# Swin block on one core: the gathers of split q and k rows move one place later, behind the next send of row maxima

## The chip, the cores and the metric

The kernel runs on one core of a Trainium2 chip. The metric is the time of one execution on the device, in microseconds. Lower is better.

## The reference

A shifted-window transformer block over an input of 8 images of 16 x 128 tokens with 32 channels. Windows are 4 x 32 tokens, so an image has 16 windows of 128 tokens; there are 4 heads of 8 channels.

```
y   = roll(layernorm(x) * g1 + b1, (-2, -2))            # then cut into windows
q, k, v = y @ qkv_w + qkv_b                             # q scaled by 8 ** -0.5
p   = softmax(q @ k.T + bias(rpb) + mask)               # 128 x 128, per window and head
x   = x + roll(p @ v @ proj_w + proj_b, (2, 2))
out = x + gelu((layernorm(x) * g2 + b2) @ fc1_w + fc1_b) @ fc2_w + fc2_b
```

All of it is float32; the gelu is the exact one.

## The kernel before

**Pairs, places and passes.** A pair is two windows with their four heads: 1024 score columns. There are 64 pairs, 8 to an image. All engines run the same loop over pairs `p` (line 285 on SyncE), written out without branches; `b = p // 8` is the image whose attention runs, and `s = p % 8` is the place in the pass of that image. Two neighbouring pairs make a group `k = j // 2`.

**Scores are computed twice.** S1 (`scores_s1`, L908) gives scores with queries on partitions; VectorE takes the maximum of every row (L524). S2 (`scores_s2`, L937) gives the transposed scores, from which ScalarE takes the exponential (L736), and TensorE multiplies that with the values (L957). S1 runs four pairs ahead of S2. So that the S2 scores come out with the row maximum already subtracted, the maxima are two more rows of the operand `q_rows`: TensorE transposes the maxima of a group (`transpose_max`, L871), ScalarE rounds them to bf16 (`m_hi`, L731), VectorE forms the remainder (`m_mid`, L530), and SyncE writes both into `q_rows` with two DMAs of 4 KB (`send_max`, L262). The S2 scores of the group's first pair wait for both DMAs (`d_m`). At every even place the loop sends group `(p + 2) // 2`; TensorE makes the transposes of that group in pair `p` just before the S2 scores of pair `p`, which belong to the group sent two places earlier. A group has thus one group's time from its transpose to its use.

**Split rows.** q and k have to be as exact as float32 but the score matmuls are bf16. So each projected q and k is split in three bf16 parts (HIGH, MID, LOW), and `q_rows` and `k_rows` hold six slots per element: on the q side three HIGH, two MID, one LOW, on the k side the same in another order. The parts of image `n` go to a scratch in HBM (`scatter`, one DMA of 256 KB for each part, L250) and come back into their slots by `gather(n, part, q or k)` (L212): three DMAs for a HIGH, two for a MID, one for a LOW, each of 128 KB. All twelve go into one of three buffers. A gather waits for the scatter of its part (`d_scr`). The first S1 scores of an image wait for all its gathers.

**SyncE's queue.** SyncE issues all of these in program order, and a wait in that order holds up everything behind it. In the pass of image `b`, the rows of image `n = b + 2` are scattered and gathered, for `n` from 2 to 7, so in passes 0 to 5. The places in that pass: 2, 4 and 6 send groups `4b + 2`, `4b + 3`, `4b + 4`; place 3 resets two rows of the buffer (`clear_max`); place 4 scatters HIGH, place 5 MID, place 6 LOW. The gathers stand at places 5, 6 and 7 and, for LOW, at place 0 of the next pass, behind the send of group `4b + 5`. Place 1 loads an image of x. Image 1 has an order of its own (pairs -2 and 0), which is not touched.

Of the kernel before, what the change touches and what calls it, by code (L numbers as in the profile page):

```python
# [19 lines left out]
HIGH, MID, LOW = 0, 1, 2  # L20
# [23 lines left out]
def swin_kernel(nc, x, params, rel_i_in, rel_j_in, aux_in, scratch, rel_scratch, out):  # L44
# [3 lines left out]
    with ExitStack() as ctx:  # L48
# [125 lines left out]
        def img(b):  # L174
            return X[:, b * IMG:(b + 1) * IMG]
# [7 lines left out]
        def low_parts(n, i):  # L183
            return 2 * n + i if n else 1
# [14 lines left out]
        def gathered(n):  # L199
            return 16 * (13 * (n // NBUF) + (12 if n % NBUF else 0))  # L200

        def gather(eng, n, part, qk):
            eng.wait_ge(d_scr[part], 16 * (n + 1))
            if n >= NBUF:
                eng.wait_ge(s2_done, PPI * (n - NBUF + 1))
            else:
                eng.wait_ge((zero_q, zero_k)[qk][n], 1)
            for s in range(6):
                if SLOT_PARTS[qk][s] == part:
                    dst = (q_rows, k_rows)[qk][s:128:8, n % NBUF, :].rearrange("p (a n) -> p a n", n=512)  # L210
                    src = scratch[n % 2, part].rearrange("u a k e n -> k e (u a) n")[qk]
                    eng.dma_start(dst, src).then_inc(d_qk[n % NBUF], 16)  # L212
# [5 lines left out]
        def _(sp):  # L218
# [11 lines left out]
            def aux_rows(i):  # L230
                lo = 0 if i else ROW // 2
                sp.wait_ge(zero_q[i], 1)
                sp.dma_start(q_rows[AUX:128:8, i, lo:].bitcast(fp32), aux_in[0, :, lo // 2:]).then_inc(d_aux[i], 16)
                sp.wait_ge(zero_k[i], 1)
                sp.dma_start(k_rows[AUX:128:8, i, lo:].bitcast(fp32), aux_in[1, :, lo // 2:]).then_inc(d_aux[i], 16)
# [8 lines left out]
            def scatter(n, part):  # L244
                if n > 2:
                    sp.wait_ge(d_qk[(n - 2) % NBUF], gathered(n - 2))
                if n == 2:
                    sp.wait_ge(d_first, 192)
                sp.wait_ge((hi_done, mid_done, lo_done)[part], low_parts(n, 1) if part == LOW else 2 * n + 2)
                sp.dma_start(scratch[n % 2, part].rearrange("u a k e n -> (a k e) u n"),  # L250
                             parts[:, n % 2, part, :, :]).then_inc(d_scr[part], 16)

            def clear_max(n):
                sp.wait_ge(s2_done, PPI * (n - NBUF + 1))
                dst = q_rows[AUX:128:32, n % NBUF, :].bitcast(fp32)
                sp.dma_start(dst, aux_in[0, 0:1, :].to_broadcast([4, ROW // 2])).then_inc(d_qk[n % NBUF], 16)

            def send_max(k):
                b, wx = k // GW, k % GW
                for at, t, done in ((AUX, m_hi, mhi_done), (AUX + 32, m_mid, mmid_done)):  # L260
                    sp.wait_ge(done, k + 1)
                    sp.dma_start(q_rows[at:128:64, b % NBUF, wx * 1024:(wx + 1) * 1024],  # L262
                                 t[:, k % 2, :]).then_inc(d_m[k % 2], 16)
# [16 lines left out]
            for p in range(FIRST, PAIRS):  # L280
                b, s = p // PPI, p % PPI
                n = b + 2
                if p % 2 == 0 and 0 <= (p + 2) // 2 < GROUPS:
                    send_max((p + 2) // 2)
                if s == 0 and 2 <= b + 1 < B:
                    gather(sp, b + 1, LOW, 0)
                    gather(sp, b + 1, LOW, 1)
                if p == -2:
                    scatter(1, HIGH)
                    scatter(1, MID)  # L290
                    gather(sp, 1, HIGH, 0)
                if p == 0:
                    scatter(1, LOW)
                    gather(sp, 1, HIGH, 1)
                    gather(sp, 1, MID, 0)
                    gather(sp, 1, LOW, 0)
                    gather(sp, 1, LOW, 1)
                if p == 3:
                    aux_rows(2)
                if s == (1 if b else 3) and b + 4 < B:  # L300
                    sp.dma_start(img(b + 4), x[:, (b + 4) * IMG:(b + 5) * IMG]).then_inc(d_x[b + 4], 16)
                if 2 <= n < B:
                    if s == 3 and n >= NBUF:
                        clear_max(n)
                    if s == 4:
                        scatter(n, HIGH)
                    if s == 5:
                        scatter(n, MID)
                        gather(sp, n, HIGH, 0)
                    if s == 6:  # L310
                        scatter(n, LOW)
                        gather(sp, n, HIGH, 1)
                    if s == 7:
                        gather(sp, n, MID, 0)
                        gather(sp, n, MID, 1)
            for m in range(B - 1):
                sp.wait_ge(res_done, m + 1)
                sp.dma_start(out[:, m * IMG:(m + 1) * IMG], res[:, m % 2, :]).then_inc(d_out[m % 2], 16)
# [929 lines left out]
```

## Time and profile before

| | us |
|---|---|
| median of 3 runs | 230.57 (229.99 to 231.49) |
| the profiled execution's own time | 228.56 |
| its span, first to last instruction | 226.8 |

| engine | busy us | share of the span |
|---|---|---|
| TensorE, matmul | 202.2 | 89% |
| VectorE | 164.7 | 73% |
| ScalarE | 149.4 | 66% |
| GpSimd | 128.3 | 57% |

The rows further down come from that one profiled execution. Times in them are microseconds from the first instruction. The loop over pairs fills about 28 to 200 us of the span; what follows is the MLP of all images.

### The profile page before, as it was taken

The page shows a single profiled execution, that of the slowest core. Times are in us where ns is not written, and L with a number is a line of the kernel's source. Part 1 is how long each engine was busy: PE and PEld are TensorE (multiplying, and loading weights), DVE is VectorE, ACT ScalarE, POOL GpSimd, SP SyncE. Part 2 cuts the span into 40 slices and gives each one's busy share as a digit, 9 for nine tenths or more (in the row PEclk, how much of TensorE's full clock was granted, in tenths as well). Part 3 has the DMA queues.
Part 4 walks back from the last instruction along what each step waited for, and adds up shares of the span by engine and source line. Part 5 has one row for each costly group of instructions (what it writes and reads, how often), then busy time and mean ns, then how long its engine had stood idle before and what let it go on. Part 6 is the DMA issues. An engine that isn't in the chain of part 4 may idle for free.

```text
span 226.8 us, 10661 instructions
## 1 busy us (share of the span) xinstructions
PE 202.2 (89%) x4600; PEld 120.9 (53%) x4600; DVE 164.7 (73%) x253; ACT 149.4 (66%) x217; POOL 128.3 (57%) x116
## 2 busy tenths in 40 slices
PE   0888789999899979997999999999969999989884
PEld 0844434655566546655665666466646666443221
DVE  3896855767688666876897887777747767866874
ACT  7465457846686656766766885857636765577883
POOL 7775698272448942987389578624651083150850
PEclk9999958999999988999999999999999999999999
DMA  6816457544523540444246224513541000000233
GB/s 206 245 55 178 123 176 221 157 135 128 173 70 97 185 143 13 138 149 145 75 153 204 66 95 128 160 57 108 155 145 31 7 4 9 1 3 0 94 140 139
DMA packets 24294, 25.57 MB, mean 113 GB/s; under 512 B 3556, under 2 KB 21732, under 8 KB 24164
## 3 DMA queue, kind: packets, MB, share of 16 engines
q1 hardware_dynamic: 23496, 24.16, 34.2%
q10 hardware_dynamic: 752, 0.74, 1.2%
q8 instruction: 36, 0.59, 1.1%
q14 instruction: 10, 0.08, 0.1%
HBM read 16.24 MB, written 8.39 MB: 109 GB/s over the span
## 4 chain that ended last, share of the span: by engine, by line
issue 40%; POOL 38%; PE 8%; DVE 5%; ACT 4%; DMA 2%; ACTq 1%; POOLq 1%; DVEq 0%
POOL rstd L376 17%; POOL X L406 4%; POOL parts L394 4%; POOL yn L386 3%; POOL xc L368 3%; POOL X L411 3%; PE ps L974 3%; DMA X<-x_tok 2%; ACT q_rows L741 1%; POOL mean L356 1%; ACT k_rows L741 1%; POOL var L362 1%; PE pq L974 1%; DVE negm L524 1%; PE pav L1004 1%
## 5 line engine op out<-in xcount | busy, mean ns | idle before, releaser
L524 DVE TENSOR_REDUCE negm<-ps 128x8 f32<-128x1024 f32 x64 | 78.1, 1223 | 30.2 <-PE ps L908 29.6
L736 ACT ACTIVATE prob<-ps 128x1024 f32<-128x1024 f32 x64 | 65.5, 1023 | 31.2 <-PE ps L937 28.9
L376 POOL TENSOR_TENSOR rstd<-var,neghalf 128x16 f32<-128x16 f32 x16 | 47.4, 2963 | 16.0 <-DVE var L489 15.1
L922 PE MATMUL ps<-rel_j,id_b 96*32 96x512 bf16 x512 | 40.6, 388 | 2.7 <-DVE negm L524 1.6
L957 PE MATMUL pav<-prob,va 128*32 128x128 f32 x1024 | 42.0, 281 | 0.5 <-issue 0.5
L937 PE MATMUL ps<-q_rows,k_rows 64*64 64x128 bf16 x1024 | 27.4, 226 | 7.2 <-DMA q_rows<-m_mid 7.1
L957 PEld LDWEIGHTS pav<-prob,va 128*32 128x32 f32 x1024 | 24.4, 110 | 13.2 <-issue 6.8
L937 PEld LDWEIGHTS ps<-q_rows,k_rows 64*64 64x64 bf16 x1024 | 16.8, 108 | 26.3 <-issue 14.9
L908 PEld LDWEIGHTS ps<-k_rows,q_rows 64*64 64x64 bf16 x1024 | 22.5, 109 | 7.0 <-issue 0.9
L908 PE MATMUL ps<-k_rows,q_rows 64*64 64x128 bf16 x1024 | 25.6, 219 | 0.0
L884 PE MATMUL ps<-rel_i,ident_b 64*64 64x512 bf16 x256 | 25.4, 386 | 0.0
L394 POOL TENSOR_TENSOR parts<-rest,parts 128x512 bf16<-128x512 f32 x15 | 17.3, 1157 | 10.5 <-ACT parts L719 10.5
L356 POOL TENSOR_SCALAR mean<-ssum 128x16 f32<-128x16 f32 x11 | 2.8, 257 | 35.9 <-DVE ssum L471 35.6
L731 ACT ACTIVATE m_hi<-pq 16x128 bf16<-16x128 f32 x32 | 8.5, 266 | 21.5 <-PE pq L871 21.0
L922 PEld LDWEIGHTS ps<-rel_j,id_b 96*32 96x32 bf16 x512 | 13.5, 98 | 6.5 <-ACT prob L736 2.9
L530 DVE TENSOR_TENSOR m_mid<-pq,m_hi 16x128 bf16<-16x128 f32 x32 | 8.7, 270 | 10.6 <-ACT m_hi L731 9.5
L386 POOL TENSOR_TENSOR yn<-xc,rstd 128x512 f32<-128x512 f32 x13 | 13.6, 1047 | 1.0
L368 POOL TENSOR_TENSOR xc<-X,mean 128x512 f32<-128x512 f32 x12 | 12.6, 1048 | 1.7 <-DVE yn L504 0.8
L471 DVE TENSOR_REDUCE ssum<-X 128x16 f32<-128x512 f32 x16 | 10.9, 680 | 3.0 <-DMA X<-x_tok 2.8
L515 DVE SCALAR_TENSOR_TENSOR rest<-pq,qk_bias,parts 128x512 f32<-128x512 f32 x12 | 9.0, 746 | 4.1 <-ACT parts L713 4.1
L483 DVE TENSOR_REDUCE vsum<-sq 128x16 f32<-128x512 f32 x16 | 10.8, 678 | 0.9 <-ACT sq L702 0.6
L1058 PE MATMUL pch<-par,oT 128*128 128x128 f32 x64 | 10.5, 286 | 1.1 <-DVE oT L626 1.1
(134 smaller groups left out, 320.1 us busy)
## 6 DMA issues: line engine op xcount, KB each, us to landing
slots<-parts SPq DMA_DIRECT2D x21, 256.0 KB, 2.9
q_rows<-slots SPq DMA_DIRECT2D x42, 128.0 KB
k_rows<-slots SPq DMA_DIRECT2D x40, 128.0 KB
X<-x_tok SPq DMA_DIRECT2D x8, 256.0 KB, 3.9
y_tok<-res SPq DMA_DIRECT2D x7, 256.0 KB, 2.0
q_rows<-m_hi SPq DMA_DIRECT2D x32, 4.0 KB
q_rows<-m_mid SPq DMA_DIRECT2D x32, 4.0 KB
bias_parts<-rel_parts SPq DMA_DIRECT2D x3, 128.0 KB
```

Of the source, the lines that this page charges most:

```text
L368: pool.tensor_tensor(per_window(xc[:, i, :]), per_window(img(n)), mean[:, i, :].unsqueeze(2).to_broadcast([128, WPI, C]), ALU.subtract).th ...
L376: pool.tensor_tensor(rstd[:, i, :], var[:, i, :], neghalf[:], ALU.pow).then_inc(rstd_done[i], 1)
L386: pool.tensor_tensor(per_window(yn[:, i, :]), per_window(xc[:, i, :]), rstd[:, i, :].unsqueeze(2).to_broadcast([128, WPI, C]), ALU.mult).t ...
L394: pool.tensor_tensor(parts[:, n % 2, LOW, u, :], rest[:, u, :], parts[:, n % 2, MID, u, :], ALU.subtract).then_inc(lo_done, 1)
L471: dve.tensor_reduce(ssum[:, i, :], per_window(img(n)), AX.X, ALU.add).then_inc(sum_done[i], 1)
L524: dve.tensor_reduce(dst, first_home(j)[:].rearrange("p (a u n) -> p a u n", u=2, n=TOK), AX.X, ALU.max, negate=True).then_inc(max_done, 1)
L736: act.activation(prob[:, j % NPROB, :], ps2[:], ACT.Exp).then_inc(exp_done, 1)
L884: pe.matmul(home[64 * c:64 * (c + 1), 512 * e:512 * (e + 1)], ident_b[64 * e:64 * (e + 1), 64 * e:64 * (e + 1)], rel_i[64 * e:64 * (e + 1) ...
L908: mm = pe.matmul(home[64 * c:64 * (c + 1), 512 * e + at:512 * e + at + TOK], q_rows[64 * e:64 * e + 64, b % NBUF, half], k_rows[64 * e:64 ...
L922: pe.matmul(ps2[32 * c:32 * (c + 1), 512 * e:512 * (e + 1)], id3_b[0:96, :], rel_j[0:96, c, e].unsqueeze(2).to_broadcast([96, 2, 2, TOK]), ...
L937: mm = pe.matmul(ps2[64 * c:64 * (c + 1), 512 * e + at:512 * e + at + TOK], k_rows[64 * e:64 * e + 64, b % NBUF, half], q_rows[64 * e:64 * ...
L957: mm = pe.matmul(pav[32 * h:32 * (h + 1), 128 * (j % 4):128 * (j % 4 + 1)], va[:, b % 2, at:at + 32], prob[:, j % NPROB, src:src + 128], s ...
```

## The change

Four `gather` calls in SyncE's loop each move to a later place. HIGH of q goes from place 5 to place 6, behind the send of group `4b + 4` and the LOW scatter. HIGH of k goes from place 6 to 7. MID of k goes from place 7 to place 0 of the next pass, behind the send of group `4b + 5` and ahead of the LOW gathers. MID of q stays at place 7. Nothing else is changed; the number of DMAs, their sizes and their waits are the same.

```diff
                 if s == 0 and 2 <= b + 1 < B:
+                    gather(sp, b + 1, MID, 1)
                     gather(sp, b + 1, LOW, 0)
                     gather(sp, b + 1, LOW, 1)
...
                     if s == 5:
                         scatter(n, MID)
-                        gather(sp, n, HIGH, 0)
                     if s == 6:
                         scatter(n, LOW)
+                        gather(sp, n, HIGH, 0)
+                    if s == 7:
                         gather(sp, n, HIGH, 1)
-                    if s == 7:
                         gather(sp, n, MID, 0)
-                        gather(sp, n, MID, 1)
```

## Rows read from the trace of the kernel before

**Rows 1.** The page: busy time by engine; granted clock in 40 slices.

```profile
PE 202.2 (89%) x4600; PEld 120.9 (53%) x4600; DVE 164.7 (73%) x253; ACT 149.4 (66%) x217; POOL 128.3 (57%) x116
...
PEclk9999958999999988999999999999999999999999
```

**Rows 2.** Waits of TensorE: who waited for whom, us in total, times, longest.

```profile
PE ps L937 <- DMA q_rows<-m_mid: 7.1, 6, 1.8
```

**Rows 3.** TensorE in order of time: start, us, instructions, [idle before <- releaser].

```profile
75.57 0.42 PE L937 MATMUL ps<-q_rows,k_rows 64*64 64x128 bf16 x16 [0.44 <-DMA q_rows<-m_mid]
...
82.47 0.42 PE L937 MATMUL ps<-q_rows,k_rows 64*64 64x128 bf16 x16 [1.58 <-DMA q_rows<-m_mid]
...
93.73 0.28 PE L871 MATMUL pq<-par,negm 128*16 128x128 f32 x1
...
105.83 0.42 PE L937 MATMUL ps<-q_rows,k_rows 64*64 64x128 bf16 x16 [1.23 <-DMA q_rows<-m_mid]
...
115.53 0.28 PE L871 MATMUL pq<-par,negm 128*16 128x128 f32 x1
...
126.13 0.28 PE L871 MATMUL pq<-par,negm 128*16 128x128 f32 x1
...
130.93 0.28 PE L871 MATMUL pq<-par,negm 128*16 128x128 f32 x1
...
136.03 0.28 PE L871 MATMUL pq<-par,negm 128*16 128x128 f32 x1
...
167.08 0.28 PE L871 MATMUL pq<-par,negm 128*16 128x128 f32 x1
```

**Rows 4.** ScalarE in order of time: `m_hi` of groups 8 and 24.

```profile
69.93 0.27 ACT L731 ACTIVATE m_hi<-pq 16x128 bf16<-16x128 f32 x1 [0.69 <-PE pq L871]
...
157.91 0.27 ACT L731 ACTIVATE m_hi<-pq 16x128 bf16<-16x128 f32 x1 [0.69 <-PE pq L871]
```

**Rows 5.** SyncE's queue in order of time, passes 0 and 1.

```profile
49.63 0.54 SPq L262 DMA_DIRECT2D q_rows<-m_hi  x1
...
51.95 2.05 SPq L212 DMA_DIRECT2D k_rows<-slots  x1
...
57.64 0.54 SPq L262 DMA_DIRECT2D q_rows<-m_hi  x1
...
70.63 2.47 SPq L212 DMA_DIRECT2D q_rows<-slots  x3
73.14 0.54 SPq L262 DMA_DIRECT2D q_rows<-m_hi  x1
...
74.38 0.37 SPq L250 DMA_DIRECT2D slots<-parts  x1
74.84 1.86 SPq L212 DMA_DIRECT2D k_rows<-slots  x3
76.80 1.19 SPq L212 DMA_DIRECT2D q_rows<-slots  x2
78.08 2.00 SPq L212 DMA_DIRECT2D k_rows<-slots  x2
80.13 0.54 SPq L262 DMA_DIRECT2D q_rows<-m_hi  x1
...
83.26 0.54 SPq L262 DMA_DIRECT2D q_rows<-m_hi  x1
```

**Rows 6.** Waits of SyncE's queue: who waited for whom, us in total, times, longest.

```profile
SPq L212 <- DMA slots<-parts: 12.7, 6, 3.4
```

**Rows 7.** Gather issues of line L212: ns least/median/most, first and last start.

```profile
L212 SPq DMA_DIRECT2D k_rows<-slots x40: 538/587/2047, 34.1 to 168.7; - x40
```

**Rows 8.** DMA queues from 51.9 to 53.0 us: packets, MB, share of 16 engines.

```profile
q8 instruction: 1, 0.02, 9.4%
```

**Rows 9.** Two stretches: us, busy by engine, granted clock, DMA share, GB/s.

```profile
76.00:80.00 4.00, 4.00 (x108) 2.37 (x104) 2.84 (x3) 3.50 (x5) 3.57 (x4) 1.00 0.56 169
83.00:87.00 4.00, 4.00 (x83) 2.32 (x75) 1.88 (x2) 1.94 (x3) 0.00 (x0) 0.57 0.42 132
```

## The prediction

> **What bounds the kernel now.** I read the page first: TensorE is busy 89% of the span, and the granted clock is full except around two places [rows 1]. So what can be won without taking work away is TensorE's idle time and the time at the lower clock. The list of what each engine waited for gives TensorE one entry of this kind inside the loop: 7.1 us in six waits of the S2 scores for the row `m_mid` of a send of row maxima [rows 2]. The order in time of TensorE [rows 3] shows three of them, two in pass 1 and one, of 1.23 us, in pass 2. Those of pass 1: 0.44 us at 75.57, for the send of group 8 (place 6 of the pass, the early send), and 1.58 us at 82.47, for the send of group 9 (place 0 of the next pass, the late send). Of the six waits this is the only one for an early send; the other five are for late sends, one in every pass with gathers but pass 3.
>
> Why the sends are late is read on ScalarE and in SyncE's queue, side by side [rows 4, 5]. `m_hi` of group 8 is finished at 70.20 (69.93 + 0.27), but its send is issued at 73.14, right behind the three gathers HIGH 0 (70.63 + 2.47). The late send goes out at 80.13, behind seven gathers and one scatter that follow the early send; TensorE reached the scores of that group at 80.89 (82.47 - 1.58) and was let go at 82.47, 2.34 us after the issue began. SyncE itself waits: 12.7 us in six waits for the scatters, ahead of HIGH 0 [rows 6]. While it waits there, the early send stands behind it.
>
> **Part 1: HIGH 0 behind the early send.** The three DMAs, and the wait on the HIGH scatter, move past two small sends and the LOW scatter on SyncE's queue. The early send then starts when `m_hi` is ready, at 70.22 and not at 73.14 in pass 1. Its 0.44 us wait goes. The scatter wait of [rows 6] costs nothing any more, because SyncE first waits for `m_hi`, and by then the scatter has had that time to land; if it has not, the rest of that wait falls between the two sends. Nothing on another engine waits for HIGH 0 soon: the gathered rows are first read by the S1 scores at place 4 of the next pass, two sends later.
>
> **Part 2: HIGH 1 and MID 1 one place later.** HIGH 1 passes no send (place 6 to place 7). MID 1, two DMAs, moves past the late send. So the run between the two sends was scatter + 3 + 2 + 2 gathers and becomes scatter + 3 + 3 + 2. Nominal steps from [rows 5]: sends and gap 73.14 to 74.38, 1.24; scatter 0.46; three gathers 1.96 (74.84 to 76.80); two gathers 1.28. Now 1.24 + 0.46 + 1.96 + 2 x 1.28 = 6.2 us; after 1.24 + 0.46 + 2 x 1.96 + 1.28 = 6.9 us. Pass 1 with the change: late send at 70.22 + 6.90 = 77.12, scores let go 2.34 later at 79.46, wanted at 80.89 - 0.44 = 80.45: **1.0 us of slack**. In passes 0 to 4 the distance between the two TensorE transposes is the same once waits are taken out, so the slack is the same. The last pass is shorter: `m_hi` ready at 158.18 (157.91 + 0.27), late send 165.1, let go 167.46, wanted at 167.08 + 0.28 = 167.36, the end of the transpose ahead of it [rows 3, 4]: 0.1 us too late even at nominal.
>
> **What eats the slack: long issues.** A gather issue takes 0.54 us at least, 0.59 in the median, but up to 2.05 [rows 7]. The interval between the sends is now 8.01, 6.99, 7.12, 6.60, 7.51 and 6.67 us in the six passes (the first two stand in [rows 5], four more are read the same way), so 1.8, 0.8, 0.9, 0.4, 1.3 and 0.5 us over nominal. HIGH 0's own three issues are over by 0.7, 0.6, 0.7, 0.5, 0.0 and 1.1 (the second is 2.47 against 1.86). The longest issue, at 51.95 [rows 5], coincides with a packet on the instruction queue [rows 8]; I found such a packet at nearly all the others. As TensorE's instruction stream does not change, these come at the same points of its work.
>
> Low end: excess as now, HIGH 0 free of it. Waits 0.8 + 0 + 0 + 0 + 0.3 + 0.6 = 1.7 us. High end: HIGH 0's excess is added to the run. Waits 1.5 + 0.4 + 0.6 + 0 + 0.3 + 1.7 = 4.5 us. I take 2.6, nearer the low end, because two of the packets that lengthen HIGH 0 (passes 0 and 5) would then fall beside the small sends, whose issues keep to 0.5 us.
>
> The Trainium skill (Runtime: NRT & Kernel Launch, "Instruction fetch mechanics") holds the crossing of an instruction block to be mostly hidden. By that the excess would vanish and the waits would be 0.1 us, which is the full case below; the 2.05 us issue speaks against it.
>
> **Part 3: what stands behind the late send.** MID 1 adds 1.28 us ahead of the next send (group 4b + 6): late send to next send is now 3.13 us (80.13 to 83.26) and becomes 4.4. Let go at 4.4 + 2.34 = 6.75 after the late send's start; TensorE, let go at 2.34 and then working one group, 4.8 us (126.13 to 130.93 [rows 3]), wants it at 7.1. It fits with 0.4 us; long issues there may take it. I put 0.3 us in all; the ends are 0 and 0.9 (a half microsecond in two passes).
>
> **Part 4: the clock.** After the 1.58 us of idleness at 80.89 the granted clock fell; in 83 to 87 us it was 0.57 of full, where the levels are 1.2 and 2.4 GHz [rows 9]. Full speed would have saved up to 4 x 0.43 = 1.7 us there. That idleness shrinks to at most 0.4 us by the sum, so I take the 1.7 back as the likelier; the other end is 0, since another long wait kept its clock. The first fall, near 28 us, is before the change's places.
>
> **Sum.** 7.1 - 2.6 - 0.3 + 1.7 = 5.9 us. It is on the path: TensorE is the busy engine, and pass 3, which has no such wait, already shows the pace without one, 20.50 us from transpose to transpose (115.53 to 136.03) against 21.80 in pass 2 (93.73 to 115.53) with a wait of 1.2 [rows 3]. So no other engine takes the place of the wait there. The profiled execution took 228.56 us (span 226.8, 1.8 around it); 228.56 - 5.9 = 222.7. The median of the runs is 2.0 above that execution, so the forecast is **224.7 us**.
>
> **Rivals.**
> - *Full gain.* No long issue in the run hits a late send: 7.1 + 1.7 = 8.8, 221.8 us. For it: 1.0 us of slack in five passes. Against: excess over 1.0 in two of the six now. Chance 0.13.
> - *Half gain.* Upper waits (4.5 + 0.9) and no clock back: 1.7 us, 228.9; with one of the two, some 227. For it: eight gathers in a row give a fetch more to hit. Chance 0.20, half of it under 1%.
> - *No change.* SyncE's order isn't what holds the scores: the waits move to the next send or to another engine. Against it pass 3. 230.6 us, chance 0.08.
> - *Slower: the send's data queue behind the gathers.* Place: the late send, with 8 gathers of 128 KB and a 256 KB scatter ahead of it, 1.31 MB in 5.7 us of issue, 230 GB/s. If they drain at only the 169 GB/s moved from 76 to 80 us [rows 9], they take 7.8 us, and the send's data land 2.1 us later. Then the waits are 2.1 + 0.9 - 1.0 = 2.0 in five passes and 3.1 in the last, 13.1 against 7.1: 236.6 us. It decides from waits above 1.2 us a pass, that is a drain below about 200 GB/s. Against it: 169 is what was issued, not what could drain, and 2.34 us from issue to release is no longer behind seven gathers than behind three (75.57 - 73.14 = 2.43). Chance 0.06. The Trainium skill (DMA: Bandwidth & Descriptors, "Queues, rings and completion order") says that descriptors of one issuing queue are consumed in ring order on each DMA engine. By that rule this would happen whenever a backlog stands; the trace shows none so far.
>
> **How the numbers follow.** Forecast 0.53, full 0.13, half 0.20, none 0.08, slower 0.06. About 1% (2.3 us) is what a measurement of this kernel tells from no change. Faster: 0.53 + 0.13 + 0.10 = 0.76. Same: 0.10 + 0.08 = 0.18. Slower: 0.06. The range reaches from the full gain, 221.8, to the upper waits without the clock, 228.9, and leaves out the last two rivals and the edges.
>
> **What would show it.** Right: in SyncE's order the early send starts within 0.1 us of `m_hi`; 6.9 to 8.5 us between the two sends; TensorE's wait for `m_mid` falls from 7.1 to about 3 us, most of it in passes 0, 4 and 5; full clock in pass 1. Wrong: a wait for `m_mid` in pass 3, more than 2.4 us from the late send to its scores, a wait of the S1 scores for gathered rows, or a clock that falls elsewhere.

## The result and the profile after

| | before | changed |
|---|---|---|
| median, us | 231.03 (229.99 to 237.69, 4 runs) | 222.96 (222.47 to 225.55, 4 runs) |
| profiled execution, us | 228.56 | 222.47 |
| its span, us | 226.8 | 220.7 |

The ratio of changed to before is 0.969, 95% interval 0.959 to 0.979 (runs that the comparison marks as disturbed are left out). In a second series on another occasion it was 0.979 (0.973 to 0.986). The change makes the kernel 2 to 3% faster; the forecast was 224.7 us, with a range from 221.8 to 228.9.

The page of the changed kernel, busy time and granted clock (against [rows 1]):

```profile
PE 199.1 (90%) x4600; PEld 119.6 (54%) x4600; DVE 165.2 (75%) x253; ACT 149.4 (68%) x217; POOL 128.4 (58%) x116
...
PEclk9999969999999999999999999999999999999999
```

The second fall of the clock is gone; the first, near 28 us and ahead of the change's places, is still there and shorter. The waits of TensorE (against [rows 2]):

```profile
PE ps L937 <- DMA q_rows<-m_mid: 4.0, 5, 1.1
```

7.1 us have become 4.0. TensorE in order of time shows where they are, with the transposes of groups 4 and 28 as marks:

```profile
41.78 0.42 PE L937 MATMUL ps<-q_rows,k_rows 64*64 64x128 bf16 x16 [0.39 <-DMA q_rows<-m_mid]
...
46.92 0.28 PE L871 MATMUL pq<-par,negm 128*16 128x128 f32 x1
...
58.51 0.42 PE L937 MATMUL ps<-q_rows,k_rows 64*64 64x128 bf16 x16 [0.72 <-DMA q_rows<-m_mid]
...
80.19 0.42 PE L937 MATMUL ps<-q_rows,k_rows 64*64 64x128 bf16 x16 [1.11 <-DMA q_rows<-m_mid]
...
142.61 0.42 PE L937 MATMUL ps<-q_rows,k_rows 64*64 64x128 bf16 x16 [0.85 <-DMA q_rows<-m_mid]
163.04 0.42 PE L937 MATMUL ps<-q_rows,k_rows 64*64 64x128 bf16 x16 [0.96 <-DMA q_rows<-m_mid]
...
172.64 0.28 PE L871 MATMUL pq<-par,negm 128*16 128x128 f32 x1
```

In the kernel before the same two marks stand here:

```profile
47.96 0.28 PE L871 MATMUL pq<-par,negm 128*16 128x128 f32 x1
...
178.73 0.28 PE L871 MATMUL pq<-par,negm 128*16 128x128 f32 x1
```

The stretch that the change touches went from 130.77 to 125.72 us, 5.05 less. Its waits went from 7.08 to 3.64 (passes 0, 1, 4 and 5; the 0.39 lies ahead of it), which is 3.44; the other 1.6 is pass 1 at full clock (1.00 from 80 to 86 us here, 0.57 from 83 to 87 in [rows 9]). The remaining 1.04 us of the span's 6.1 was gained ahead of the mark, where no wait of TensorE was touched. It does not belong to the change: in the second profile of the changed kernel, further down, the first mark stands at 48.49, later than before.

SyncE's queue in pass 1 (against [rows 5]):

```profile
68.81 0.52 SPq L262 DMA_DIRECT2D q_rows<-m_hi  x1
69.38 0.51 SPq L262 DMA_DIRECT2D q_rows<-m_mid  x1
70.00 0.36 SPq L250 DMA_DIRECT2D slots<-parts  x1
70.46 3.33 SPq L212 DMA_DIRECT2D q_rows<-slots  x3
73.89 1.84 SPq L212 DMA_DIRECT2D k_rows<-slots  x3
75.83 1.96 SPq L212 DMA_DIRECT2D q_rows<-slots  x2
77.83 0.54 SPq L262 DMA_DIRECT2D q_rows<-m_hi  x1
78.42 0.54 SPq L262 DMA_DIRECT2D q_rows<-m_mid  x1
79.06 1.21 SPq L212 DMA_DIRECT2D k_rows<-slots  x2
```

The early send starts at 68.81, 0.02 us after `m_hi` is ready. The late send starts 9.0 us after it, not 6.9: HIGH of q took 3.33 us for three issues (1.86 nominal) and MID of q 1.96 for two (1.19). The scores were let go at 80.19, 2.36 us after the late send's start. SyncE's wait for scatters ahead of a gather, 12.7 us in [rows 6], is now:

```profile
SPq L212 <- DMA slots<-parts: 0.3, 1, 0.3
```

### The profile page after: what moved, and what is told of

Same layout as the page of the kernel before. It is cut to its first block, busy times and chain, and to the rows that moved or that the text cites. A ratio compares the mean times of both kernels' runs of the same rounds, so it can differ in the third digit from the quotient of the medians.

```text
span 220.7 us, 10661 instructions
## 1 busy us (share of the span) xinstructions
PE 199.1 (90%) x4600; PEld 119.6 (54%) x4600; DVE 165.2 (75%) x253; ACT 149.4 (68%) x217; POOL 128.4 (58%) x116
## 4 chain that ended last, share of the span: by engine, by line
issue 38%; POOL 37%; PE 9%; ACT 5%; DMA 4%; DVE 4%; SPq 1%; ACTq 1%; POOLq 1%; DVEq 0%
POOL rstd L376 17%; POOL X L406 5%; POOL parts L394 3%; POOL yn L386 3%; POOL X L411 3%; POOL xc L368 3%; PE ps L974 3%; DMA slots<-parts 2%; DMA X<-x_tok 2%; ACT q_rows L741 2%; POOL mean L356 1%; ACT k_rows L741 1%; POOL var L362 1%; PE pq L974 1%; ACTq L193 1%
## 5 line engine op out<-in xcount | busy, mean ns | idle before, releaser
L922 PE MATMUL ps<-rel_j,id_b 96*32 96x512 bf16 x512 | 39.8, 381 | 2.7 <-DVE negm L524 1.6
L957 PE MATMUL pav<-prob,va 128*32 128x128 f32 x1024 | 41.5, 279 | 0.1
L957 PEld LDWEIGHTS pav<-prob,va 128*32 128x32 f32 x1024 | 24.2, 109 | 12.7 <-issue 6.2
L937 PE MATMUL ps<-q_rows,k_rows 64*64 64x128 bf16 x1024 | 26.9, 223 | 4.1 <-DMA q_rows<-m_mid 4.0
## 6 DMA issues: line engine op xcount, KB each, us to landing
q_rows<-slots SPq DMA_DIRECT2D x42, 128.0 KB
k_rows<-slots SPq DMA_DIRECT2D x40, 128.0 KB
bias_parts<-rel_parts SPq DMA_DIRECT2D x3, 128.0 KB
```

The source lines that it names most:

```text
L922: pe.matmul(ps2[32 * c:32 * (c + 1), 512 * e:512 * (e + 1)], id3_b[0:96, :], rel_j[0:96, c, e].unsqueeze(2).to_broadcast([96, 2, 2, TOK]), ...
L937: mm = pe.matmul(ps2[64 * c:64 * (c + 1), 512 * e + at:512 * e + at + TOK], k_rows[64 * e:64 * e + 64, b % NBUF, half], q_rows[64 * e:64 * ...
L957: mm = pe.matmul(pav[32 * h:32 * (h + 1), 128 * (j % 4):128 * (j % 4 + 1)], va[:, b % 2, at:at + 32], prob[:, j % NPROB, src:src + 128], s ...
```

## The experiments

The theory: SyncE issues in order, each gather ahead of a send delays it by its issue time, and TensorE waits for what exceeds the slack of one group. The rivals: the early send was what mattered; the sends' data queue behind the gathers; long issues belong to a place in the run of DMAs and not to instruction fetches; the gain is the clock's.

**HIGH of q alone** (the other two moves left out of the change; HIGH of k, which passes no send, was not tried by itself):

```diff
                     if s == 5:
                         scatter(n, MID)
-                        gather(sp, n, HIGH, 0)
                     if s == 6:
                         scatter(n, LOW)
+                        gather(sp, n, HIGH, 0)
                         gather(sp, n, HIGH, 1)
```

> Kernel before, with only HIGH of q moved: behind the early send and the LOW scatter. Theory (each DMA that SyncE issues ahead of a send delays the scores by its issue time): the early send is free, so its wait of 0.44 us goes; but the run between the two sends is now 1.24 + 0.46 + 2 x 1.96 + 2 x 1.28 = 8.2 us, and the late send comes 0.61 + 8.2 + 2.34 = 11.1 us after the transpose against 10.9 wanted: 0.3 us short in passes 0 to 4 even without long issues, 1.4 in pass 5. With 0.4 to 1.8 us of long issues a pass the late waits come to 6 to 9 us in six passes, pass 3 among them. Time 228 to 232, the same as before within 1%. Rival (it was the early send, held by the scatter wait, that cost the time): most of the gain of the whole change, 223 to 225 us, and TensorE's wait for m_mid under 4 us.

Measured: 233.5 us median, ratio to before 1.030 (1.016 to 1.043). Its waits of TensorE, and the one in pass 3, which had none before:

```profile
PE ps L937 <- DMA q_rows<-m_mid: 8.6, 6, 2.4
```

```profile
124.30 0.42 PE L937 MATMUL ps<-q_rows,k_rows 64*64 64x128 bf16 x16 [0.99 <-DMA q_rows<-m_mid]
```

The waits are in the range expected, the median is above it. The rival, which asked for 223 to 225 us and waits under 4 us, falls. How much slower the kernel became is less certain: its two fastest runs took 229.6 and 231.7 us, 1.4% more on average than the four fastest of the kernel before, run beside it (225.8 to 229.1), and the trace has 1.5 us more of waits (8.60 against 7.08).

**MID of k alone:**

```diff
                 if s == 0 and 2 <= b + 1 < B:
+                    gather(sp, b + 1, MID, 1)
                     gather(sp, b + 1, LOW, 0)
...
                     if s == 7:
                         gather(sp, n, MID, 0)
-                        gather(sp, n, MID, 1)
```

> Kernel before, with only MID of k moved behind the late send; both HIGH gathers stay. Theory: the late send starts 1.28 us earlier in every pass, so of the late waits of before (1.07, 1.58, 1.23, 0, 1.00, 1.76) 0.3 and 0.5 us are left, and the early wait of 0.44 stays: about 1.2 us for m_mid in all. Time 222 to 225 us, no slower than the whole change and perhaps 1 us faster. Rival (the early send's freedom is needed, because late waits start from a late early send): late waits stay above 4 us, 226 us or more.

Measured: 220.8 us median, ratio 0.971 (0.963 to 0.979). TensorE's waits, in order:

```profile
37.21 0.42 PE L937 MATMUL ps<-q_rows,k_rows 64*64 64x128 bf16 x16 [0.43 <-DMA q_rows<-m_mid]
42.89 0.42 PE L937 MATMUL ps<-q_rows,k_rows 64*64 64x128 bf16 x16 [1.12 <-DMA q_rows<-m_mid]
...
105.10 0.42 PE L937 MATMUL ps<-q_rows,k_rows 64*64 64x128 bf16 x16 [0.24 <-DMA q_rows<-m_mid]
...
160.89 0.42 PE L937 MATMUL ps<-q_rows,k_rows 64*64 64x128 bf16 x16 [0.23 <-DMA q_rows<-m_mid]
```

Between the marks 0.6 us is left (a third wait, 0.11 us in pass 0, isn't shown); the first two lie ahead. The time is better than the 222 to 225 us expected. So the move of MID of k, two DMAs a pass, is enough for the whole gain. HIGH of q cost SyncE little where it stood, since SyncE had nothing else to do between the MID scatter and the early send. Moved, it stands in the run that has no time to spare.

**LOW ahead as well** (kernel before, one more part ahead of the late send):

```diff
                 if s == 0 and 2 <= b + 1 < B:
-                    gather(sp, b + 1, LOW, 0)
-                    gather(sp, b + 1, LOW, 1)
...
                         gather(sp, n, MID, 1)
+                        gather(sp, n, LOW, 0)
+                        gather(sp, n, LOW, 1)
```

> Kernel before, with the two LOW gathers put ahead of the late send as well, so one part more of what the change takes away: 1.28 us of issue is added to the run between the sends. Theory: the late waits of passes 0, 1, 2, 4 and 5 each grow by 1.28 us and pass 3 gets one of 0.7, so TensorE waits 7.1 + 7.1 = 14 us for m_mid; the span grows from 226.8 to about 234, and by up to 1.7 us for each fall of the granted clock that the longer idleness brings. The issue of the late send's first DMA to the release of the scores stays at 2.3 us. Rival (data queue on the DMA rings behind the gathers): that last time grows with nine gathers ahead, to 3 us or more, and the waits with it beyond 14 us.

Measured: 240.8 us in one run, span 239.0. Its late waits in the six passes, and its clock:

```profile
62.73 0.42 PE L936 MATMUL ps<-q_rows,k_rows 64*64 64x128 bf16 x16 [3.26 <-DMA q_rows<-m_mid]
86.29 0.42 PE L936 MATMUL ps<-q_rows,k_rows 64*64 64x128 bf16 x16 [1.43 <-DMA q_rows<-m_mid]
...
110.00 0.42 PE L936 MATMUL ps<-q_rows,k_rows 64*64 64x128 bf16 x16 [3.14 <-DMA q_rows<-m_mid]
...
132.70 0.42 PE L936 MATMUL ps<-q_rows,k_rows 64*64 64x128 bf16 x16 [0.61 <-DMA q_rows<-m_mid]
156.37 0.64 PE L936 MATMUL ps<-q_rows,k_rows 64*64 64x128 bf16 x16 [3.10 <-DMA q_rows<-m_mid]
...
179.94 0.64 PE L936 MATMUL ps<-q_rows,k_rows 64*64 64x128 bf16 x16 [2.83 <-DMA q_rows<-m_mid]
```

```profile
PEclk9999959999889999998899999979997999999999
```

They add up to 14.4 us, 0.61 in pass 3 among them; expected were 14 and 0.7. The sum was met, the spread was not: by the same 1.28 us on each, pass 1 was to have 2.9 us and has 1.43, and passes 0, 2 and 4 have 0.6 to 0.9 more than that. From the late send's first issue to the release it took 2.22 to 2.32 us in five passes and 2.68 in one, behind nine gathers, where the rival asked for 3 us or more: the data do not queue to an extent that shows. The span was 5 us above the 234 expected, which the clock accounts for: it fell at each of the four waits of 2.8 us or more.

**Another phase of TensorE's instruction fetches** (changed kernel):

```diff
+            for _ in range(128):
+                pe.wait_ge(w_ready, 1)
             pe.wait_ge(w_ready, 1)
```

> Changed kernel, with 128 more wait instructions on a semaphore that is already up, put at the head of TensorE's program, where TensorE waits for the weights anyway; nothing else differs. They shift the points at which TensorE's instruction stream needs its next block by half a block, some 2.2 us of its work. Theory (long issues on SyncE come from these fetches): the long issues move with the packets of the instruction queue, so the waits for m_mid are spread differently from 0.72, 1.11, 0, 0, 0.85, 0.96 us over the six passes: the long second HIGH issue of pass 1 (2.07 us, at 71.09) is short or elsewhere, and the sum comes to 2 to 4.5 us. Time within 2 us of the changed kernel. Rival (the long issues belong to a place in the run of DMAs, by a backlog): the same issues are long as in the changed kernel, and the waits keep their passes within 0.2 us.

Measured: 227.4 us in one run. The added waits were not free at the head: TensorE's first matmul started at 13.54 us, at 6.71 in the changed kernel, so the expected time was missed by the head. Between the marks, however, it took 124.1 us, less than the changed kernel. All its waits there:

```profile
110.51 0.42 PE L937 MATMUL ps<-q_rows,k_rows 64*64 64x128 bf16 x16 [0.18 <-DMA q_rows<-m_mid]
127.61 0.42 PE L937 MATMUL ps<-q_rows,k_rows 64*64 64x128 bf16 x16 [1.44 <-DMA q_rows<-m_mid]
167.99 0.42 PE L937 MATMUL ps<-q_rows,k_rows 64*64 64x128 bf16 x16 [0.42 <-DMA q_rows<-m_mid]
```

SyncE's gathers in pass 1, and then those in pass 3:

```profile
76.39 1.94 SPq L212 DMA_DIRECT2D q_rows<-slots  x3
78.43 1.83 SPq L212 DMA_DIRECT2D k_rows<-slots  x3
80.36 1.19 SPq L212 DMA_DIRECT2D q_rows<-slots  x2
...
117.65 3.48 SPq L212 DMA_DIRECT2D q_rows<-slots  x3
121.23 1.83 SPq L212 DMA_DIRECT2D k_rows<-slots  x3
123.15 2.07 SPq L212 DMA_DIRECT2D q_rows<-slots  x2
```

Pass 1, which held the longest issue of the changed kernel (2.07 us, in HIGH of q), is clean. The same pattern now stands in pass 3, where one issue of 0.97 us stood between the sends. That is not chance from one execution to the next: the second profile of the changed kernel has it in pass 1 again, with 2.09 us for the same issue:

```profile
71.25 3.35 SPq L212 DMA_DIRECT2D q_rows<-slots  x3
```

A packet of the instruction queue q8, which moves 0.59 MB of the 0.67 MB of instructions, starts 2.86 us after the transpose of group 8 in the changed kernel and 2.82 us after it in its second profile; here it starts 1.33 us after. SyncE's program is the same in all three, so the place in the run does not make an issue long; when TensorE fetches does. The records agree: in all nine traces, 96 gather issues after 42 us took over 0.75 us, and every one overlaps a packet of q8. Of the 557 shorter ones 76 do. None of these issues was long without a fetch, then, but a fetch doesn't always lengthen one. By what way a fetch reaches SyncE's issue stays open.

**Both MID gathers behind the late send,** HIGH where it was, x one place later; with the changed kernel and MID of k alone once more, on one chip:

```diff
                 if s == 0 and 2 <= b + 1 < B:
+                    gather(sp, b + 1, MID, 0)
+                    gather(sp, b + 1, MID, 1)
...
-                if s == (1 if b else 3) and b + 4 < B:
+                if s == (2 if b else 3) and b + 4 < B:
...
-                    if s == 7:
-                        gather(sp, n, MID, 0)
-                        gather(sp, n, MID, 1)
```

> Kernel before, with both MID gathers behind the late send and the load of x one place later (behind the send of group 4b + 6); HIGH stays where it was. Theory (SyncE's issue time between sends is all that counts): the run from early to late send falls to 1.24 + 0.46 + 1.96 = 3.7 us and the one to the next send is 1.23 + 3 x 1.28 = 5.1, both shorter than a group's time on TensorE, so no wait for m_mid is left in passes 0 to 5, long issues or not. From the transpose of group 4 to that of group 28 it takes 122.0 us at full clock (before 130.8, changed 125.7, MID of k alone 122.5). Time 219 to 221 us, level with MID of k alone within 1%. Rival (gathered rows come too late for the S1 scores, as four gathers more are issued after the late send): a wait of the S1 scores on a gather appears, 222 us or more.

> The changed kernel itself, beside the two others on one chip. Theory: 222 to 224 us, 2 to 4.5 us of waits for m_mid; slower than MID of k alone by 1 to 3 us, because HIGH of q now stands in the run between the two sends, where SyncE has no idle time, instead of ahead of the early send, where it had some. Rival (the difference came from the clock alone, which stayed full in the one profile of MID of k alone): level within 0.5 us.

> Only MID of k behind the late send, as run before, beside the changed kernel on one chip. Theory: 220 to 222 us, under 1 us of waits in passes 0 to 5. Rival: as for the changed kernel.

| kernel | median, us | ratio to before | between the marks, us | DMA waits there, us | rest, us |
|---|---|---|---|---|---|
| before (first profile) | 231.03 | | 130.77 | 7.08 | 123.7 |
| changed | 222.96 | 0.969 (0.959 to 0.979) | 125.72 | 3.64 | 122.1 |
| HIGH of q alone | 233.52 | 1.030 (1.016 to 1.043) | 132.34 | 8.60 | 123.7 |
| MID of k alone | 220.81 | 0.971 (0.963 to 0.979) | 122.50 | 0.58 | 121.9 |
| LOW ahead | 240.79 | | 142.39 | 14.37 | 128.0 |
| other phase | 227.40 | | 124.06 | 2.04 | 122.0 |
| both MID | 222.13 | 0.973 (0.967 to 0.979) | 122.44 | 0.61 | 121.8 |
| changed again | 223.58 | 0.979 (0.973 to 0.986) | 125.45 | 3.51 | 121.9 |
| MID of k alone again | 222.94 | 0.976 (0.969 to 0.982) | 124.60 | 2.63 | 122.0 |

The 3.51 of the changed kernel again holds 0.65 us that is not for `m_mid` (below). Where the clock stayed full between the marks, the rest is 121.8 to 122.1 us whatever the order: the waits are the whole difference. Before and HIGH of q alone hold one clock fall there, LOW ahead four. The expectation of no wait for both MID gathers was nearly met (0.47 and 0.14 are left, on early sends), and the S1 scores do not wait there, as its rival had it; its median is 1.1 us above the 219 to 221 expected. That of under 1 us for MID of k alone was met once and missed once, with 1.18 us in pass 5, and its 222.9 us lies above the 220 to 222 expected. The intervals of the last three ratios overlap; that MID of k alone beats the changed kernel is likely by the traces, but its lead beside it is 0.6 us where 1 to 3 were expected, and the ratios do not settle it.

Part 3's fear came true once. In the second profile of the changed kernel, the first S1 scores of image 5, at place 4 of pass 4, waited 0.65 us for its gathered rows; no other of the nine profiles lists such a wait. The last gather was issued at 123.92, the scores started at 128.12:

```profile
123.92 0.54 SPq L212 DMA_DIRECT2D k_rows<-slots  x1
```

```profile
128.12 0.42 PE L908 MATMUL ps<-k_rows,q_rows 64*64 64x128 bf16 x16 [0.65 <-DMA k_rows<-slots]
```

## Why the prediction was right, point by point

- **Mechanism and sign: right.** Six sends were late for SyncE's queue; the gathers in front of them were the reason. The forecast gain of 5.9 us stands against 6.1 in the profiled executions, but by a partly different sum: waits 3.4 (4.2 forecast, with part 3), clock 1.6 (1.7), and 1.0 ahead of the first mark that has nothing to do with the change. That the two sums agree so closely is luck. The median, 222.96 us, came out 1.7 below the forecast, mostly because the forecast put it 2.0 us above the profiled execution, as in the kernel before, and here it is 0.5 above.
- **Part 1: the step is right, its worth was misread.** The early send starts 0.61 us after its transpose in all six passes. But "a wait that costs nothing any more" hid that the idle time had paid for HIGH of q's issues. By itself the move adds 1.5 us of waits; I had it as a gain of 0.44 us and its price only inside part 2's longer run.
- **Part 2: right in the nominal run.** Passes 2 and 3 show 7.3 and 7.2 us between the sends, one long issue of 0.4 in each: 6.9 without. The slack held: no wait in these two.
- **Long issues: right in kind, low in size.** 2.6 us were taken, 3.6 measured, inside the ends of 1.7 and 4.5. Passes 0, 4 and 5 got 0.72, 0.85 and 0.96, each inside its ends or within 0.6 of them; pass 1 got 1.11 where at most 0.4 was given, because HIGH of q, now in the run, met a fetch for 1.5 us and MID of q another for 0.8. Reading the excess off the places of before could not see that; the fetches had to be laid against the new order. The Trainium skill (Runtime: NRT & Kernel Launch, "Instruction fetch mechanics") calls such crossings mostly hidden. TensorE's own stream agrees: between the marks of the changed kernel 26 packets of q8 start, and its only idle times of 0.15 us or more are the four waits for `m_mid`. The cost shows on SyncE.
- **Part 3: right for the next send** (none of the waits of the first profile is there, one of 0.42 in the second); the S1 scores have less room than "two sends later" suggested, as shown above.
- **Part 4: as forecast, but not shown to be caused.** The 1.7 us were taken back because pass 1 was to idle at most 0.4 us; it idled 1.11 and kept full clock all the same, so this term came out by luck. Runs at full clock from first to last exist of the kernel before (227.6 us) and, beside it, of the changed one (222.6): 5.0 us apart, so most of the gain needs no clock.
- **The slower rival: refuted.** Where TensorE waited, it took 2.24 to 2.44 us from late send to release behind eight gathers, 2.22 to 2.43 before. The ring order that the Trainium skill states (DMA: Bandwidth & Descriptors, "Queues, rings and completion order") would need a backlog to cost time; with 2.7 us at most, behind nine gathers, no run here shows one.
- **The signs named beforehand: not all came.** Between the two sends lie 9.0 and 8.9 us in passes 1 and 4, above the 8.5 given. The 2.44 us of pass 0, from late send to release, is a hair above the 2.4 named. The second profile shows two more of the signs of being wrong, the S1 wait and a wait of 0.42 us in pass 3; both come from long issues behind the late send, and the order of the gathers still explains them.

## What to carry to other kernels

Where one queue issues both bulk transfers and small urgent ones, count its issue time between two urgent ones and compare it with the time in which their result is wanted; here the bytes between them did not show in the result. Put bulk issues where the queue is idle, even ahead of an urgent one that has slack, and take them out of the run that has none. Test each moved piece by itself: here one of them lost part of what another won.

## What was not expected of the hardware

A gather issue on SyncE, 0.59 us in the median, took up to 2.2 us while a packet of the instruction queue q8 was under way, and a shift of TensorE's program by 128 instructions changed which issues were hit. The granted clock fell from its upper level (2.4 GHz) to its lower one (1.2 GHz) at four waits of TensorE of 3.26, 3.14, 3.10 and 2.83 us (LOW ahead), after one of 1.58 (the kernel before) and after one of 2.45 (HIGH of q alone). It stayed full after waits of 1.76 (the kernel before) and 1.92 (HIGH of q alone), and after all waits of 1.44 us and less between the marks. What decides between these cases is not shown.
